# An audio tower on one core: three of five token tiles get their 128th-largest value by a bit search

## The chip, the cores and the metric

The kernel runs on 1 core of one Trainium2 chip. The metric is device microseconds for one launch over all 32 sequences; lower is better. Three runs of the kernel before took 9348.07, 9358.02 and 9363.74 us, median 9358.02. An engine is named as in the profile: PE (TensorE), PEld (its weight loads), DVE (VectorE), ACT (ScalarE), POOL (GpSimd), SP (the DMA queue).

## The reference

For each of 32 sequences of 80000 samples, 625 frames of 128 samples (padded to 626) go through a DCT and three residual blocks:

```
h = dct(frames)
h = h + bidirectional_mamba2(layernorm(h))        # 4 heads x 64, state 16, sequential scan over 626 steps
h = h + moe(layernorm(h))                         # 8 experts, top 2, hidden 512, gelu
h = h + window_attention(layernorm(h))            # 8 shifts, softmax over the shifts
h = h + sparse_ffn(layernorm(h))
```

and the last one, which the change touches, is

```
a1 = gelu(x @ ipT)            # 512 values;  keep the 64 largest, others 0
a2 = gelu(a1_kept @ pwT)      # 256 values;  keep the 128 largest, softmax over those kept
v  = softmax_kept @ pv        # 64 values
a3 = gelu(v @ owT)            # 512 values;  keep the 64 largest, others 0
out = a3_kept @ op
```

All in float32.

## The kernel before

A sequence is 626 tokens, in five tiles of 128 tokens (`TILES`). Work on one sequence is cut in three stages: stage 1 is DCT and the scan block, stage 2 the experts and the attention, stage 3 the sparse feed-forward block. The loop is a software pipeline over sequences: one pass does stage 1 of sequence b, stage 2 of b-1 and stage 3 of b-2; two passes ahead of it and two behind it are partial. Each engine's part of a stage is a generator that yields between steps, and a string of digits for each engine (`PE_ORDER`, `ACT_ORDER`, `DVE_ORDER`, `POOL_ORDER`) says, digit by digit, which stage's generator takes its next step. The order of work on an engine is therefore fixed by hand; engines meet only through semaphores, and an engine that waits holds all that stands behind it in its string.

What the change and the prediction touch:

- `take_top` (lines 1017 to 1034) picks the k largest of a row on DVE: each round is a MAX8 (line 1028, the eight largest) and a MATCH_REPLACE8 (line 1030, those eight overwritten), preceded by a small MATCH_VALUE_LOAD. 64 of 512 takes 8 rounds, 128 of 256 takes 16. Tiles go in groups of three and two; rounds of the tiles of a group alternate. It runs three times: on `a1` (K1 = 64), on `a2` (K2 = 128) and on `a1` again (K3 = 64). `select` (line 1039) then zeroes what was not taken; for `a2` line 1068 does that and sums the row.
- ACT in stage 3: the evacuations and Gelus of lines 794 to 821, and one Exp per tile (line 807). In stage 2 ACT makes 64 Gelus per sequence (line 768) between PE's first (line 564) and second (line 575) expert products; PE can be only two halves ahead of ACT.
- POOL: layer norms (lines 312 to 317), and the attention's softmax and value sums. Those are few and wide: line 369 subtracts over 5120 columns in one instruction, lines 373, 376 and 392 add over 2560, 1280 or 640 columns.
- The scan block of stage 1 has 12 steps (lines 474 to 497, 742, 894 to 905). In each, PE multiplies `Bw` with `Cs` (16 rows, 121 weight columns, line 474) and transposes two 128 x 121 pieces of `xs` (line 481), both into 121 partitions, makes the skip and the head products (lines 491, 497), and DVE scans (line 894) and weighs (lines 902, 905).

## Time and profile before

| | |
|---|---|
| median of 3 runs | 9358.02 us |
| the profiled execution | 9383.6 us |
| its span, first to last instruction | 9381.6 us |
| busy: DVE / PE / ACT / POOL | 8440.0 / 7197.0 / 3228.9 / 2332.9 us |
| mean granted PE clock | 0.792 |

A busy time is the sum of the engine's instructions in the span; the chain of waits is the path of work, followed back from the last instruction, that ended last. The granted clock is given as a share of 2.4 GHz: 1.00 is 2.4 GHz and 0.50 is 1.2 GHz.

### The profile page before, as it was taken

The numbers are of one execution on the slowest core, as the hardware profiler recorded it, in microseconds if no ns is written. First come the engines' busy times: TensorE is split into PE (matmuls) and PEld (weight loads), VectorE is DVE, ScalarE is ACT, GpSimd is POOL, SyncE is SP. The second block draws the span as 40 slices with busy tenths as digits, with TensorE's granted clock in tenths as the row PEclk, the third lists the DMA queues.
The fourth block names the chain that finished last, engine by engine and source line by source line (L and its number), as shares of the span: only waits on it lengthen the run. The fifth ranks groups of instructions, "written<-read, shape, count | busy, mean of one in ns | idle before, by whom it ended". The sixth has DMA issues, their size and how long they took to land.

```text
span 9381.6 us, 113931 instructions
## 1 busy us (share of the span) xinstructions
PE 7197.0 (77%) x35336; PEld 5130.3 (55%) x35336; DVE 8440.0 (90%) x23276; ACT 3228.9 (34%) x5649; POOL 2332.9 (25%) x1967
## 2 busy tenths in 40 slices
PE   6778787787787787877777877878877878777773
PEld 4555555555565565555555555555555555555552
DVE  2699989989999999998999899999989999989998
ACT  2233333333333333333333333333333343333331
POOL 1332212332122322123322223221233222232220
PEclk9778877778887788787788777787877888778875
DMA  1000000000000000000000000000000000000000
GB/s 53 14 16 14 6 12 16 16 16 11 5 16 16 16 14 6 12 16 16 16 14 4 14 16 16 14 8 10 16 16 16 14 6 12 16 16 16 10 5 3
DMA packets 95339, 128.48 MB, mean 14 GB/s; under 512 B 7600, under 2 KB 94096, under 8 KB 94096
## 3 DMA queue, kind: packets, MB, share of 16 engines
q1 hardware_dynamic: 94736, 120.71, 4.8%
q8 instruction: 345, 5.65, 0.3%
q14 instruction: 258, 2.11, 0.1%
HBM read 109.68 MB, written 11.01 MB: 13 GB/s over the span
## 4 chain that ended last, share of the span: by engine, by line
DVE 59%; PE 26%; issue 7%; ACT 4%; POOL 3%; DMA 0%; DVEq 0%; SPq 0%; POOLq 0%; ACTq 0%
DVE m L1028 17%; DVE work L1030 14%; PE pM L575 6%; PE pM L564 6%; DVE dtw L870 4%; DVE a L1030 3%; PE pS L497 3%; PE pS L491 3%; DVE a L1039 2%; DVE h L972 2%; DVE hid L982 2%; ACT hid L768 2%; PE pS L481 2%; DVE hid L993 2%; DVE stats L853 2%
## 5 line engine op out<-in xcount | busy, mean ns | idle before, releaser
L1030 DVE MATCH_REPLACE8 work<-m,work 128x256 f32<-128x256 f32 (+1 forms) x4192 | 2178.7, 537 | 0.0
L1028 DVE MAX8 m<-work 128x8 f32<-128x256 f32 (+1 forms) x4192 | 2035.1, 539 | 1.0
L564 PE MATMUL pM<-uT,cst 128*128 128x320 f32 x4096 | 1495.2, 493 | 313.3 <-ACT hid L768 173.5
L768 ACT ACTIVATE hid<-pM,cst 128x320 f32<-128x320 f32 x2048 | 1060.3, 528 | 1247.8 <-PE pM L564 641.8
L463 PE MATMUL pS<-u_fm,wconv_s 128*128 128x315 f32 (+1 forms) x3072 | 1027.7, 496 | 498.6 <-DVE dtw L870 380.8
L575 PEld LDWEIGHTS pM<-cst,hid 128*128 128x128 f32 x10240 | 1185.8, 191 | 125.9 <-DVE h L972 80.6
L564 PEld LDWEIGHTS pM<-uT,cst 128*128 128x128 f32 x4096 | 724.2, 206 | 967.9 <-ACT hid L768 784.2
L575 PE MATMUL pM<-cst,hid 128*128 128x128 f32 x10240 | 1204.8, 275 | 49.1 <-DVE h L972 47.2
L312 POOL TENSOR_TENSOR rstd<-vare,mhalf 128x5 f32<-128x5 f32 x160 | 187.4, 1171 | 4171.8 <-DVE vare L859 4171.8
L463 PEld LDWEIGHTS pS<-u_fm,wconv_s 128*128 128x128 f32 (+1 forms) x3072 | 585.8, 196 | 953.3 <-DVE dtw L870 398.4
L497 PE MATMUL pS<-Mt,Xw 121*64 121x121 f32 x3072 | 359.2, 376 | 313.8 <-DVE Mt L905 313.7
L742 ACT COPY xs<-pS 128x242 f32<-128x242 f32 x384 | 138.9, 362 | 1297.3 <-PE pS L497 1297.3
L1028 DVE MAX8 m<-a 128x8 f32<-128x512 f32 x768 | 507.4, 682 | 86.2 <-issue 83.3
L894 DVE TENSOR_TENSOR_SCAN ab<-ab,cst 121x488 f32<-121x488 f32 x384 | 552.0, 1437 | 20.3 <-DMA ab<-decay_rows 19.2
L369 POOL TENSOR_TENSOR hid<-hid,red 128x5120 f32<-128x5120 f32 x32 | 350.7, 10960 | 710.5 <-DVE red L988 710.5
L340 POOL TENSOR_TENSOR yg<-xs,zs 128x525 f32<-128x525 f32 (+1 forms) x256 | 194.4, 799 | 1137.8 <-ACT xs L742 1107.4
L972 DVE SCALAR_TENSOR_TENSOR h<-pM,lgt,h 128x128 f32<-128x128 f32 x1280 | 361.6, 353 | 105.9 <-PE pM L575 100.2
L497 PEld LDWEIGHTS pS<-Mt,Xw 121*64 121x64 f32 x3072 | 233.0, 191 | 383.3 <-DVE Mt L905 320.2
L1030 DVE MATCH_VALUE_LOAD work<-m,work 128x8 f32 x4192 | 380.7, 91 | 0.0
L902 DVE TENSOR_TENSOR Xw<-pS,dts 121x256 f32<-121x256 f32 x384 | 159.2, 415 | 236.7 <-PE pS L481 236.2
L392 POOL TENSOR_TENSOR hid<-hid 128x2560 f32<-128x2560 f32 (+2 forms) x96 | 344.0, 3583 | 54.2 <-DVE hid L993 49.0
L1030 DVE MATCH_REPLACE8 a<-m,a 128x512 f32<-128x512 f32 x512 | 349.6, 683 | 0.0
(193 smaller groups left out, 12223.9 us busy)
## 6 DMA issues: line engine op xcount, KB each, us to landing
ab<-decay_rows SPq DMA_DIRECT2D x384, 230.7 KB
x_sb<-in_x SPq DMA_DIRECT2D x32, 256.0 KB
out<-hk SPq DMA_DIRECT2D x32, 256.0 KB
cst<-in_weights SPq DMA_DIRECT2D x2, 2048.0 KB, 12.0
hid<-in_setup SPq DMA_DIRECT2D x1, 1904.0 KB, 20.9
out<-hk SPq DMA_DIRECT2D x32, 57.0 KB
x_sb<-in_x SPq DMA_DIRECT2D x32, 56.5 KB
cst<-in_weights SPq DMA_DIRECT2D x1, 1344.0 KB, 17.0
```

The lines of the kernel that those rows point to most:

```text
L369: nc.gpsimd.tensor_tensor(lg, lg, red[:, 0:1, :].broadcast_to((P, AW, W)), ALU.subtract).then_inc(G["lg_done"].s, 1)
L392: nc.gpsimd.tensor_tensor(lg[:, 0:n, :], lg[:, 0:n, :], lg[:, n:2 * n, :], ALU.add).then_inc(G["val_tree"].s, 1)
L463: last = nc.tensor.matmul(pS[0:rows, 512 * (n % 3):512 * (n % 3) + HQ], wt, tap(d, i, half * HQ, HQ), start=(j == 0), stop=(j == len(block ...
L497: last = nc.tensor.matmul(pS[r * HD:(r + 1) * HD, B2 + g * WIN:B2 + (g + 1) * WIN], Xw[d][:, hh, :], Mt[d][:, hh, :], start=False, stop=(g ...
L564: nc.tensor.matmul(pM[:, 512 * (n % 2):512 * (n % 2) + W // 2], w1[:, e, j * P:(j + 1) * P], uT[:, lo:lo + W // 2], start=True, stop=True) ...
L575: last = nc.tensor.matmul(pM[:, B2 + P * (m % 4):B2 + P * (m % 4 + 1)], hid[:, e % 2, j, tok(t)], w2[:, e, j, :], start=(j == 0), stop=(j ...
L768: nc.scalar.activation(hid[:, e % 2, j, lo:lo + W // 2], pM[:, 512 * (n % 2):512 * (n % 2) + W // 2], ACT.Gelu, bias=c("b1")[:, n // 2:n / ...
L870: nc.vector.scalar_tensor_tensor(dtw[:, 1, :], dtw[:, 0, :], -1.0, dtw[:, 0, :], ALU.mult, ALU.max).then_inc(G["dt_arg"].s, 1)
L894: nc.vector.tensor_tensor_scan(decays, decays, c("scan_src", WIN), 0.0, ALU.mult, ALU.add).then_inc(G["scanned"].s, 1)
L972: last = nc.vector.scalar_tensor_tensor(h2[:, t, :], pM[:, B2 + P * (m % 4):B2 + P * (m % 4 + 1)], gate[:, t, e:e + 1], h2[:, t, :], ALU.m ...
L1028: link(nc.vector.max(m[i], now[i]), len(tiles) - 1)
L1030: link(nc.vector.match_replace(work[i], m[i], now[i], GONE), len(tiles) - 1 if r or firsts is None else 0)
```

## The change

`e2` now stands for tiles 3 and 4 only; tiles 0 to 2 (`SEARCHED = 3`) do not go through the 16 rounds on `a2`. For these three, a fourth generator, `search`, on ACT and POOL finds the 128th-largest value of each row bit by bit. In a turn, ACT makes three Sign passes over 257 columns (one per tile, sign of `flip * a2 + guess`, the sum of the signs into `below`), and POOL answers with three small instructions on 128 x 3 integers that set or leave a bit of `guess`. There are 31 turns and a few passes more before and after (Square passes that count ties, an upper neighbour of the value). DVE then makes the mask from the marks: a scan that numbers the ties, a compare-and-add, and the masked product that was there before. The search has the digit 4 in the orders; all four orders are new.

```diff
+SEARCHED = 3
+BITS = 31
+TURN = (3, 4, 0, 1, 2)
-            for tiles in groups:
-                dve.wait_ge(G["a2_sb"].s, G["a2_sb"](b, tiles[-1] + 1))
-                yield from take_top(tiles, a2, K2, halves, best)
+            for t in there:                                   # tiles 0, 1, 2
+                last = nc.vector.max(best[:, t, :], a2[:, t, 0:NP_])
+            ...
+            yield from take_top(here, a2[:, :, 0:NP_], K2, halves, best)      # tiles 3, 4
+            ...
+            for t in there:
+                dve.wait_ge(G["missing"].s, G["missing"](b, 1))
+                dve.wait_ge(G["e2s"].s, G["e2s"](b, t + 1))
+                link(nc.vector.tensor_tensor_scan(untied[:, t, :], c("minus1").broadcast_to((P, NP_)), untied[:, t, :], 0.0, ALU.add, ALU.add))
+                link(nc.vector.scalar_tensor_tensor(untied[:, t, :], untied[:, t, :], missing[:, t:t + 1], marks[:, t, 0:NP_], ALU.is_ge, ALU.add))
+                link(nc.vector.scalar_tensor_tensor(a2[:, t, 0:NP_], untied[:, t, :], 1.0, a2[:, t, 0:NP_], ALU.is_ge, ALU.mult,
+                                                    accum_out=rsum[:, t:t + 1]))
```

A turn on ACT, and its answer on POOL:

```diff
+            for n in range(BITS + 1):
+                yield
+                act.wait_ge(G["guess"].s, G["guess"](b, n + 2))
+                for t in range(SEARCHED):
+                    last = nc.scalar.activation(marks[:, t, :], a2[:, t, :], ACT.Sign, scale=flip[:, t:t + 1], bias=guess_f[:, t:t + 1],
+                                                accum_out=below[:, 0, t:t + 1])
+                last.then_inc(G["counted" if n < BITS else "marks"].s, 1)
```

```diff
+            for n in range(BITS):
+                yield
+                pool.wait_ge(G["counted"].s, G["counted"](b, n + 2))
+                wide = 1 << (BITS - 1 - n)
+                nc.gpsimd.tensor_tensor(raised[:], guess[:], halves_i[:, n:n + 1].broadcast_to((P, SEARCHED)), ALU.add)
+                nc.gpsimd.tensor_scalar(bit[:], below[:, 0, :], 1.0, float(wide), ALU.is_ge, ALU.mult).then_inc(G["tried"].s, 1)
+                pool.wait_ge(G["tried"].s, G["tried"](b, n + 1))
+                nc.gpsimd.tensor_tensor(guess[:], raised[:], bit[:], ALU.subtract).then_inc(G["guess"].s, 1)
```

Stage 3 now goes through its second half twice, first for tiles 3 and 4 and then for 0, 1 and 2 (`TURNS`). The wide POOL instructions of the attention become one instruction per 640 columns (8, 4, 2 and 4 + 2 + 1 of them):

```diff
-            nc.gpsimd.tensor_tensor(lg, lg, red[:, 0:1, :].broadcast_to((P, AW, W)), ALU.subtract).then_inc(G["lg_done"].s, 1)
+            for w in range(AW):
+                last = nc.gpsimd.tensor_tensor(lg[:, w, :], lg[:, w, :], red[:, 0, :], ALU.subtract)
+            last.then_inc(G["lg_done"].s, 1)
```

In the scan block `Bw` has 128 columns and the transposed pieces of `xs` too, so that these three PE products of a step write 128 partitions, where 121 are used:

```diff
-                nc.tensor.matmul(pS[0:WIN, at:at + WIN], Bw[d][:, ch, :], Cs[d][:, ch, :], start=True, stop=True)
+                nc.tensor.matmul(pS[:, at:at + WIN], Bw[d][:, ch, :], Cs[d][:, ch, :], start=True, stop=True)
-                    last = nc.tensor.transpose(pS[0:WIN, at + P + g * P:at + P + (g + 1) * P], xs[d][:, g, ch * WIN:(ch + 1) * WIN], ident)
+                    last = nc.tensor.transpose(pS[:, at + P + g * P:at + P + (g + 1) * P], xs[d][:, g, ch * WIN:ch * WIN + P], ident)
```

The new orders, cut to their first digits where they are long:

```
ACT_ORDER   278 digits (243 before), of them 41 fours, the first after 35 twos (16 of the 64 expert Gelus), the 32nd after 121
POOL_ORDER  "2334444444444141444444444444444444444444242222211222121141"
DVE_ORDER   119 digits (132 before)
PE_ORDER    227 digits (225 before)
```

## Rows read from the trace of the kernel before

**Rows 1.** The page: busy time of each engine.
```profile
PE 7197.0 (77%) x35336; PEld 5130.3 (55%) x35336; DVE 8440.0 (90%) x23276; ACT 3228.9 (34%) x5649; POOL 2332.9 (25%) x1967
```

**Rows 2.** The page: the chain that ended last, by engine and by line.
```profile
DVE 59%; PE 26%; issue 7%; ACT 4%; POOL 3%; DMA 0%; DVEq 0%; SPq 0%; POOLq 0%; ACTq 0%
DVE m L1028 17%; DVE work L1030 14%; PE pM L575 6%; PE pM L564 6%; DVE dtw L870 4%; DVE a L1030 3%; PE pS L497 3%; PE pS L491 3%; DVE a L1039 2%; DVE h L972 2%; DVE hid L982 2%; ACT hid L768 2%; PE pS L481 2%; DVE hid L993 2%; DVE stats L853 2%
```

**Rows 3.** Timeline, POOL's first instruction of stage 3 (start us, us).
```profile
392.36 1.25 POOL L400 TENSOR_TENSOR hk<-h,zero 128x640 f32<-128x640 f32 x1
...
8959.39 1.25 POOL L400 TENSOR_TENSOR hk<-h,zero 128x640 f32<-128x640 f32 x1
```

**Rows 4.** Windows of one pass: start:end length, PE, PEld, DVE, ACT, POOL busy, PEclk, DMA, GB/s.
```profile
4302.90:4326.90 24.00, 13.57 (x63) 9.66 (x61) 23.92 (x25) 4.23 (x9) 19.33 (x8) 0.81 0.06 21
...
4375.00:4399.10 24.10, 14.83 (x56) 9.75 (x56) 14.24 (x64) 6.29 (x10) 17.88 (x26) 0.65 0.06 16
...
sum 288.60, PE 225.51 PEld 161.49 DVE 264.04 ACT 101.00 POOL 72.79; mean PE 18.79 PEld 13.46 DVE 22.00 ACT 8.42 POOL 6.07
```

**Rows 5.** Windows: the expert stage of one pass, and the scan steps.
```profile
4094.00:4234.00 140.00, 113.63 (x588) 82.16 (x586) 127.45 (x456) 56.16 (x101) 12.41 (x18) 0.87 0.01 3
...
4326.00:4362.00 36.00, 35.98 (x180) 28.38 (x181) 26.46 (x44) 4.46 (x12) 0.16 (x1) 0.50 0.25 62
```

**Rows 6.** Groups by form: one replace per tile and round, 256 columns.
```profile
L1030 DVE MATCH_REPLACE8 work<-m,work 128x256 f32<-128x256 f32 x2400 | 975.6, 428 | 0.0
```

**Rows 7.** DVE timeline: two successive rounds of three tiles begin.
```profile
4175.80 1.07 DVE L1028 MAX8 m<-work 128x8 f32<-128x256 f32 x3
...
4177.96 1.07 DVE L1028 MAX8 m<-work 128x8 f32<-128x256 f32 x3
```

**Rows 8.** Timeline: DVE instructions beside wide POOL instructions, and without them.
```profile
4142.71 0.69 DVE L1039 SCALAR_TENSOR_TENSOR a<-work,a 128x512 f32<-128x512 f32 x1
...
4266.60 10.96 POOL L369 TENSOR_TENSOR hid<-hid,red 128x5120 f32<-128x5120 f32 x1 [22.42 <-DVE red L988]
4266.67 10.96 DVE L870 SCALAR_TENSOR_TENSOR dtw<-dtw 121x48 f32<-121x48 f32 x1
...
4282.96 0.21 DVE L884 SCALAR_TENSOR_TENSOR dts<-dtw 121x48 f32<-121x48 f32 x1
...
4299.76 3.23 DVE L1039 SCALAR_TENSOR_TENSOR a<-work,a 128x512 f32<-128x512 f32 x1
...
4315.42 4.35 DVE L894 TENSOR_TENSOR_SCAN ab<-ab,cst 121x488 f32<-121x488 f32 x1
...
4327.85 1.17 DVE L894 TENSOR_TENSOR_SCAN ab<-ab,cst 121x488 f32<-121x488 f32 x1
```

**Rows 9.** ACT timeline: three Exp passes of stage 3.
```profile
4188.60 1.31 ACT L807 ACTIVATE a<-a,nmax 128x256 f32<-128x256 f32 x3
```

**Rows 10.** Groups by form, ACT: a pass with and without a scale vector, table loads, Square.
```profile
L768 ACT ACT_TABLE_LOAD x94 | 120.6, 1283 | 3.7 <-PE pM L575 2.0
L817 ACT ACTIVATE a<-pD,rsum 128x512 f32<-128x512 f32 x160 | 109.9, 687 | 361.5 <-PE pD L658 361.1
L794 ACT ACTIVATE a<-pD 128x512 f32<-128x512 f32 x160 | 91.8, 595 | 200.8 <-PE pD L623 200.8
L747 ACT ACTIVATE zs<-yg 128x1280 f32<-128x1280 f32 x64 | 81.4, 1272 | 85.4 <-POOL yg L340 85.4
```

**Rows 11.** Groups by form: small POOL instructions, and the read of DVE's accumulator.
```profile
L312 POOL TENSOR_TENSOR rstd<-vare,mhalf 128x5 f32<-128x5 f32 x160 | 187.4, 1171 | 4171.8 <-DVE vare L859 4171.8
L315 POOL TENSOR_TENSOR tick_pool<-zero 128x1 f32<-128x1 f32 x160 | 39.9, 249 | 12.5
L392 POOL TENSOR_TENSOR hid<-hid 128x640 f32<-128x640 f32 x32 | 49.7, 1555 | 2.5
L1068 DVE DVE_READ_ACCUMULATOR a<-work,a 128x1 f32 x160 | 14.7, 92 | 0.0
```

More of the change, by code:

```diff
@@ L10 @@
 U32 = mybir.dt.uint32
+I32 = mybir.dt.int32
 AX = mybir.AxisListType
@@ L391, in pool_stage2 @@
                 pool.wait_ge(G["val_tree"].s, G["val_tree"](b, j + 1))
-                nc.gpsimd.tensor_tensor(lg[:, 0:n, :], lg[:, 0:n, :], lg[:, n:2 * n, :], ALU.add).then_inc(G["val_tree"].s, 1)
+                for w in range(n):
+                    last = nc.gpsimd.tensor_tensor(lg[:, w, :], lg[:, w, :], lg[:, w + n, :], ALU.add)
+                last.then_inc(G["val_tree"].s, 1)
             yield
@@ L818, in act_stage3 @@
-            for t in range(TILES):
-                yield
-                act.wait_ge(G["oT_ps"].s, G["oT_ps"](b, t + 1))
-                nc.scalar.copy(selT[:], pD[:, 0:512]).then_inc(G["oT_sb"].s, 1)
+                nc.scalar.activation(a2[:, t, 0:NP_], pD[:, 512:512 + NP_], ACT.Gelu).then_inc(G["a2_sb"].s, 1)
+            for i, t in enumerate(TURN[0:TILES - SEARCHED]):
+                yield
+                act.wait_ge(G["top2"].s, G["top2"](b, TILES))
+                nc.scalar.activation(a2[:, t, 0:NP_], a2[:, t, 0:NP_], ACT.Exp, bias=nmax[:, t:t + 1]).then_inc(G["e2"].s, 1)
@@ L1044, in select, with out @@
                 yield
-                dve.wait_ge(done.s, done(b, tiles[-1] + 1))
-            def out(t):
+                dve.wait_ge(done.s, done(b, first + len(tiles)))
+            def out(i):
                 yield
-                dve.wait_ge(G["fin_ps"].s, G["fin_ps"](b, t + 1))
+                dve.wait_ge(G["fin_ps"].s, G["fin_ps"](b, i + 1))
+                t = TURN[i]
                 nc.vector.tensor_tensor(hk[:, t, :], hk[:, t, :], pD[:, 512:512 + P], ALU.add).then_inc(G["out_sb"].s, 1)
-            groups = [range(0, 3), range(3, TILES)]
@@ L1053, in dve_stage3 @@
-            for tiles in groups:
+            here, there = range(SEARCHED, TILES), range(0, SEARCHED)
+            for tiles in (there, here):
                 yield
                 dve.wait_ge(G["a1_sb"].s, G["a1_sb"](b, tiles[-1] + 1))
-                yield from take_top(tiles, a1, K1, places(TILES - 2))
-                yield from select(tiles, places(TILES - 2), G["sel1"])
+                yield from take_top(tiles, a1, K1, places(SEARCHED))
+                yield from select(tiles, places(SEARCHED), G["sel1"], tiles[0])
@@ L1085, in dve_stage3 @@
-            for t in due:
-                yield from out(t)
+            yield
+            dve.wait_ge(G["a2_sb"].s, G["a2_sb"](b, SEARCHED))
+            nc.vector.memset(tick[:], 0.0)
+            for t in there:
+                last = nc.vector.max(best[:, t, :], a2[:, t, 0:NP_])
+            link(last)
+            nc.vector.tensor_scalar(nmax[:, 0:SEARCHED], best[:, 0:SEARCHED, 0], -1.0, None, ALU.mult).then_inc(G["top2"].s, SEARCHED)
+            yield
+            dve.wait_ge(G["a2_sb"].s, G["a2_sb"](b, TILES))
@@ L1087, in dve_stage3 @@
+            yield
+            dve.wait_ge(G["h3_kept"].s, G["h3_kept"](b, 1))
+            for i in range(len(here)):
+                yield from out(i)
+            yield
+            dve.wait_ge(G["a3_sb"].s, G["a3_sb"](b, TILES))
+            yield from take_top(there, a1, K3, places(SEARCHED))
+            yield from select(there, places(SEARCHED), G["sel3"], len(here))
+            for i in range(len(here), TILES):
+                yield from out(i)
             dve.sem_clear(link3)
```

276 lines of the change are left out of this document (174 added, 102 removed).

## The prediction, written before the changed kernel was run

> **What bounds the kernel now.** I read the page's busy times first [rows 1]: DVE is busy 90% of the span, PE 77%, ACT 34%, POOL 25%. The chain of waits says the same [rows 2]: 59% DVE, above all the two top-k instructions (17% and 14%), and 26% PE. So DVE bounds, with PE not far behind. Next the period: stage 3's first POOL instruction comes at 392.36 us for the first sequence and at 8959.39 for the 31st, so one pass takes 8567.0 / 30 = 285.6 us [rows 3]; the window of one pass that I cut is 288.6 long, with DVE busy 264.0, PE 225.5, ACT 101.0, POOL 72.8 [rows 4]. Then the stages of a pass. In the expert stage (140 us) DVE is busy 127.5, PE 113.6, ACT only 56.2 [rows 5]. In the scan steps PE is busy 35.98 of 36 us, at a granted clock of 0.50 (1.2 GHz), and DVE has 9.5 us of gaps. In the norms between blocks DVE is busy 14.2 of 24.1 us [rows 4]. Last, DVE's own time hides waits: a 121 x 48 instruction takes 10.96 us, exactly beside POOL's 10.96 us subtraction, where its like takes 0.21 us [rows 8]. The trace calls that busy.
>
> **The change part by part**, per pass.
>
> *Top-k on DVE.* 2400 replaces of 256 columns with 75 per sequence are five tiles by 15 rounds, and a first round reads `a2` [rows 6]. A round of three tiles starts every 4177.96 - 4175.80 = 2.16 us [rows 7]. Sixteen rounds: 34.6 us. Three MAX8 stay, 1.1 us. Removed: 33.5 us. Added for three tiles: a scan over 256 columns, at the undisturbed 1.17 us for 488 [rows 8] 0.61 us, and one compare-and-add over 256, about half of 0.69 us for 512 plus its start, 0.42; with the links 1.1 us a tile, 3.4 us. Net -30 us (both ends: 3 tiles at 0.9 to 1.8 us, so -31 to -28).
>
> *POOL in 640-column pieces.* What waits beside wide POOL instructions in a pass [rows 8]: line 870, 10.96 - 0.21 = 10.75; line 1039, 3.23 - 0.69 = 2.5 and 1.3 in the next one; a scan, 4.35 - 1.17 = 3.2. Sum 17.8 us. With pieces a DVE instruction can wait at most for the piece in front, 10.96 / 8 = 1.37 to 1.55 us [rows 11]. Perhaps three of them do and lose 0.7 to 1.5 us each. Gain 14 us, bounds 8 and 17. PE's projections, which stand behind line 870, start 9 us sooner with it. POOL pays: 21 pieces at 1.55 instead of 1.37 us are 4 us, in a POOL busy for a quarter of the time, beside DVE's top-k rounds; without that cover the attention is 4 us later.
> By the Trainium skill (GPSIMD Engine Reference, Key points) GpSimd shares its SBUF interfaces with VectorE instructions that have two SBUF inputs, and the trace agrees: MAX8 rounds beside POOL keep their time, line 870 (two inputs) does not. If that held for each small piece too, every two-input instruction in those 12 us would pay one piece, and the gain would be the 8 us above.
>
> *The search, on ACT.* Three passes over 256 columns with a bias vector take 1.31 us [rows 9]. A scale vector adds 687 - 595 = 92 ns to a pass [rows 10]; an accumulator read takes 92 ns on DVE [rows 11], and ACT's is not shown, bounds 0 and 0.3 us per pass. A turn's passes: 1.31 + 3 x 0.092 + 3 x 0.092 = 1.86 us, bounds 1.6 and 2.5. There are 36 groups of three passes: 67 us. ACT goes from 101 to 168 of some 255 us.
>
> *The search, on POOL.* A turn is three instructions with one wait between. The smallest two-input one takes 249 ns, the power on 128 x 5 takes 1171 ns [rows 11]. An integer add on 128 x 3 is no power; I take 0.25 each and 0.1 for each of two hand-overs and the wait, 1.05 us; bounds 0.8 and 3.7. A turn is then 1.86 + 1.05 = 2.9 us, bounds 2.4 and 6.2. 31 turns: 90 us.
>
> *Where the turns stand.* In ACT's order they lie among the expert Gelus, from the 16th to the 59th: 43 of 64. At the 140 us of the whole stage (in part before and after the Gelus, which take some 128 us) 43 Gelus took about 86 us. Thirty-one turns need 90, and the Gelus and copies between them (43 x 0.53 = 23 us and 5 us) fill POOL's answers, 31 x 1.05 = 33 us. ACT waits for POOL in a turn and holds Gelus behind it, for which PE waits. So the expert stage, where the removed rounds stood, does not get shorter: it stays at about 140 us. What shortens is the rest, as tile work of DVE can move into the stage's freed 30 us.
>
> *The rest of the pass* is 285.6 - 140 = 145.6 us. PE is busy 225.5 - 113.6 = 112 us in it. DVE has 264.0 - 127.5 = 136.5 in it; minus 14 (POOL) and minus up to 30 of moved work it has 93 to 100. So PE bounds the rest, at 112 us if packed without gaps; it had 33 us of gaps. I give it 3 us of gaps: 115.
>
> *128 columns in the scan steps.* Seven more columns per load and 48 such products a pass: under 1 us more. Whether the fuller products lift the clock of 0.50 no row shows: bounds +1 and -10 us (twelve steps of 3.25 us would fall to DVE's 2.2 us and hand-overs, 2.4). I take 0, the row that is: PE was already busy 35.98 of 36 us and still at 0.50 [rows 5], so seven in 128 columns is a small push.
> The Trainium skill (TensorE: Matmul & The Clock Gate, Part 4) says that a transpose does not count as busy time for the clock; two of the three widened products of a step are transposes. By it the widening gives nothing; without it the 10 us of the bound are open.
>
> *Sum.* Period 140 + 115 = 255 us, 30.6 less than 285.6. Thirty such passes: -918 us. The ends: the passes with stages 1 and 2 only, and 2 and 3 only, lose their POOL waits and some rounds, -30 us; the last stage 3 stands alone, took 182 us, and now has K1 (30), 33 turns (90), scan, weights and third product (25), K3 (30) and the outputs in a row, about +10. Profiled execution: 9383.6 - 918 - 20 = 8446 us. The median of the runs lies 25.6 us below the profiled time: 8420 us.
>
> **The rivals.**
> *Clock.* The widened products lift the scan steps to 1.00. Period 246, 8150 us. For it: all else in those steps is dense. Against: the row above.
> *The chain of stage 3.* The first half of stage 3, 33 turns in a row, then the second half for three tiles make one dependent chain: 30 + 10 + 95 + 25 + 30 + 10 = 200 us, without the waits in line for DVE and PE that others hold. If those cost another 70, the chain is the bound, and half of the gain is given back: period 271, some 8910 us. For it: the norm stretch shows DVE gaps of 10 us in 24 [rows 4] that are such chains. Against: the orders are free to put it first.
> *Slower: the turn.* The ladder decides from the point at which 31 turns outlast the 90 us by the 30.6 us gained, a turn of 3.9 us. That happens if the three POOL steps are like the power of 1171 ns (a turn of 5.4 us) or if a Sign pass needs another table than the Gelus around it: two loads of 1.28 us [rows 10] for a turn, 5.5 us. Either adds 78 us to the expert stage: period 333 us, 10800 us. Against: Square and the copies run behind any table without a load of their own at their lines [rows 10], and the power is the one slow POOL instruction.
> The Trainium skill (ScalarE: Activation LUTs, Table sets) says that cheap functions are in every set and names relu, copy, identity and abs; it does not name Sign there, though it gives Sign the same accuracy class as those. By the rule the loads stay away.
> *It moves nothing*: DVE's 44 us go and PE's waits take their place, all of them. PE has 60 us of gaps in a pass [rows 4], so this needs every gap to stay.
>
> **How the numbers follow.** The forecast has 0.55 (its own range 8250 to 8640), the clock 0.13, the stage-3 chain with half of the gain 0.20, no change 0.02, slower 0.10. A change of under 0.2%, 19 us, can't be told from none. Faster: 0.88, same 0.02, slower 0.10. The range that leaves out two in ten reaches from the clock case, 8120, to most of the chain case, 8850.
>
> **What would show it.** DVE busy falls to about 220 us a pass, lines 1028 and 1030 at 256 columns to two fifths; line 870 falls under 2 us. ACT's Sign groups of three take about 1.9 us and no table load stands before them; POOL's answer is about 1 us; ACT is busy 165 to 170 us a pass. The expert stage keeps its 140 us, the rest falls to 115. PE is busy over 85%, and the chain of waits has more PE than DVE. The scan steps stay at 0.50 and 3.2 us each. Wrong if a turn is over 3.9 us, if loads stand in front of the Sign passes, or if the granted clock in the scan steps rises.

## The result, and the profile after

The changed kernel takes 9048.24 us (median of 4 runs, 9036.43 to 9059.44) against 9357.11 before (4 runs, 9348.07 to 9363.74): a ratio of 0.967, 95% interval 0.9654 to 0.9687. It is faster, as forecast, but by 309 us and not by 937: 8420 was predicted, and 9048 lies outside the range that ended at 8850.

The page of the changed kernel, span and busy times, and the shares of the chain that ended last; they answer to [rows 1] and [rows 2].

```profile
span 9034.6 us, 123676 instructions
...
PE 6831.5 (76%) x35336; PEld 4900.9 (54%) x35336; DVE 6980.2 (77%) x18956; ACT 5064.2 (56%) x12534; POOL 3220.1 (36%) x5905
...
issue 30%; DVE 27%; PE 24%; POOL 13%; ACT 5%; POOLq 1%; DMA 0%; ACTq 0%; SPq 0%; DVEq 0%
```

Read it beside the forecast. DVE lost 1460 us, 45.6 a sequence; the 44 that were forecast are there. ACT gained 1835 us, 57 a sequence where 67 were forecast. But no engine is busy more than 77% of the span (PE was to be over 85%), and the chain has 30% "issue", time in which an engine waits for nothing that the profile shows. No single engine bounds the whole of this kernel.

The timeline of POOL's first instruction of stage 3, first and 31st sequence, in answer to [rows 3]:

```profile
370.94 1.25 POOL L431 TENSOR_TENSOR hk<-h,zero 128x640 f32<-128x640 f32 x1
...
8562.93 1.25 POOL L431 TENSOR_TENSOR hk<-h,zero 128x640 f32<-128x640 f32 x1
```

(8562.93 - 370.94) / 30 = 273.1 us a pass, 12.5 less than the 285.6 before, where 30.6 were forecast. One pass in two windows, from POOL's first instruction of stage 3 to the end of the last query, key and value product, which is called the expert stage here, and the rest (start:end length, busy us of PE, PEld, DVE, ACT, POOL, granted clock, DMA share, GB/s), in answer to [rows 4, 5]:

```profile
4193.38:4357.56 164.18, 131.74 (x680) 94.16 (x679) 125.50 (x404) 127.11 (x339) 32.86 (x123) 0.93 0.00 1
4357.56:4466.46 108.90, 80.20 (x428) 57.83 (x427) 92.50 (x188) 30.87 (x52) 67.86 (x61) 0.75 0.12 34
sum 273.08, PE 211.94 PEld 151.99 DVE 218.00 ACT 157.99 POOL 100.73; mean PE 105.97 PEld 75.99 DVE 109.00 ACT 78.99 POOL 50.36
```

Cut at the same places, a pass of the kernel before (4102.20 to 4391.78) has 151.9 and 137.7 us. Its passes differ, so the means over 27 passes of each trace say more: 150.6 and 135.0 us before, 164.2 and 108.9 now. (The prediction's window of 140 us lay a little differently.) So the rest shortened by 26 us, not far from the 30.6 forecast, and the expert stage, which was to keep its length, grew by 14. Inside the stage, windows of 21 us show who was short there:

```profile
4256.40:4277.40 21.00, 17.11 (x107) 13.62 (x106) 8.30 (x33) 19.23 (x57) 9.30 (x31) 1.00 0.00 0
4277.40:4298.40 21.00, 18.70 (x104) 14.04 (x104) 20.93 (x89) 19.64 (x56) 4.20 (x21) 0.92 0.01 2
4298.40:4319.40 21.00, 17.78 (x82) 10.39 (x80) 6.05 (x25) 19.91 (x55) 3.18 (x16) 1.00 0.00 1
```

ACT is busy 19.2 to 19.9 of 21 us while DVE falls to 8.3 and 6.1. An engine at 56% over the span is at 91 to 95% in these 63 us of the pass. Two turns back to back, ACT's timeline (start, us):

```profile
4241.57 0.53 ACT L843 ACTIVATE hid<-pM,cst 128x320 f32<-128x320 f32 x1
4242.30 0.60 ACT L909 ACTIVATE marks<-a,guess,flip 128x257 f32<-128x257 f32 x1 [0.21 <-POOL guess L449]
4242.81 0.19 ACT L909 ACTIVATION_READ_ACCUMULATOR marks<-a,guess,flip 128x1 f32 x1
4242.90 0.59 ACT L909 ACTIVATE marks<-a,guess,flip 128x257 f32<-128x257 f32 x1
4243.39 0.19 ACT L909 ACTIVATION_READ_ACCUMULATOR marks<-a,guess,flip 128x1 f32 x1
4243.49 0.59 ACT L909 ACTIVATE marks<-a,guess,flip 128x257 f32<-128x257 f32 x1
4243.98 0.19 ACT L909 ACTIVATION_READ_ACCUMULATOR marks<-a,guess,flip 128x1 f32 x1
4244.07 0.92 ACT L843 ACTIVATE hid<-pM,cst 128x320 f32<-128x320 f32 x2
4244.95 0.60 ACT L909 ACTIVATE marks<-a,guess,flip 128x257 f32<-128x257 f32 x1
```

A group of three takes 1.77 us, a turn here 2.65 us, and two Gelus fit exactly into POOL's answer: the turn is as forecast (2.9), and better packed. What it does to the Gelus shows in where the 64 of one pass stand, before and after (first and last start, us):

```profile
L768 ACT ACTIVATE hid<-pM,cst x64: 519/527/569, 4132.3 to 4224.4; 128x320 f32<-128x320 f32 x64
```
```profile
L843 ACT ACTIVATE hid<-pM,cst x64: 502/522/534, 4213.1 to 4334.2; 128x320 f32<-128x320 f32 x64
```

They took 92 us and now take 121. PE waits for them; the groups of PE's first expert product before and after (busy us, mean ns, idle us before and its releasers):

```profile
L564 PE MATMUL pM<-uT,cst 128*128 128x320 f32 x4096 | 1495.2, 493 | 313.3 <-ACT hid L768 173.5 <-DVE h L963 95.5
```
```profile
L636 PE MATMUL pM<-uT,cst 128*128 128x320 f32 x4096 | 1578.2, 503 | 617.2 <-ACT hid L843 481.3 <-DVE h L1072 117.3
```

The wait for ACT's Gelus, `hid`, was 173.5 us over the run, at 181 places; now it is 481.3, at 488.

### The profile page after: what moved, and what is told of

It reads as the page before. It is cut to its first block, busy times and chain, and to the rows that moved or that the text cites. A ratio compares the mean times of both kernels' runs of the same rounds, so it can differ in the third digit from the quotient of the medians.

```text
span 9034.6 us, 123676 instructions
## 1 busy us (share of the span) xinstructions
PE 6831.5 (76%) x35336; PEld 4900.9 (54%) x35336; DVE 6980.2 (77%) x18956; ACT 5064.2 (56%) x12534; POOL 3220.1 (36%) x5905
## 4 chain that ended last, share of the span: by engine, by line
issue 30%; DVE 27%; PE 24%; POOL 13%; ACT 5%; POOLq 1%; DMA 0%; ACTq 0%; SPq 0%; DVEq 0%
PE pS L535 8%; DVE m L1137 8%; DVE work L1139 5%; DVE a L1139 3%; POOL bit L447 3%; PE pM L636 2%; PE pD L710 2%; POOL raised L446 2%; POOL guess L449 2%; DVE ab L1003 2%; POOL u L339 1%; PE pM L647 1%; DVE red L1106 1%; PE pS L569 1%; DVE stats L962 1%
## 5 line engine op out<-in xcount | busy, mean ns | idle before, releaser
L636 PE MATMUL pM<-uT,cst 128*128 128x320 f32 x4096 | 1578.2, 503 | 617.2 <-ACT hid L843 481.3
L909 ACT ACTIVATE marks<-a,guess,flip 128x257 f32<-128x257 f32 x3072 | 1809.8, 592 | 230.9 <-POOL guess L449 194.8
L1139 DVE MATCH_REPLACE8 work<-m,work 128x512 f32<-128x512 f32 (+1 forms) x2752 | 1580.8, 581 | 0.0
L1137 DVE MAX8 m<-work 128x8 f32<-128x512 f32 (+1 forms) x2752 | 1499.1, 585 | 1.1
L446 POOL TENSOR_TENSOR raised<-guess,halves 128x3 int32<-128x3 int32 x992 | 206.2, 208 | 2238.4 <-ACT marks L909 2238.4
L535 PE MATMUL pS<-u_fm,wconv_s 128*128 128x315 f32 (+1 forms) x3072 | 868.5, 433 | 5.5 <-ACT Cs L804 5.5
L393 POOL TENSOR_TENSOR hid<-hid,red 128x640 f32<-128x640 f32 x256 | 518.9, 2059 | 606.7 <-DVE red L1097 606.7
L895 ACT COPY selT<-pD 128x512 f32<-128x512 f32 x160 | 93.8, 586 | 983.9 <-PE pD L742 983.2
L909 ACT ACTIVATION_READ_ACCUMULATOR marks<-a,guess,flip 128x1 f32 x3072 | 577.3, 188 | 0.0
L742 PE MATMUL pD<-cst,a 128*128 128x128 f32 x640 | 137.5, 354 | 432.0 <-DVE a L1148 385.6
L422 POOL TENSOR_TENSOR hid<-hid 128x640 f32<-128x640 f32 x224 | 338.6, 1536 | 173.6 <-DVE hid L1102 168.5
```

Source lines behind the costliest of these rows:

```text
L393: last = nc.gpsimd.tensor_tensor(lg[:, w, :], lg[:, w, :], red[:, 0, :], ALU.subtract)
L446: nc.gpsimd.tensor_tensor(raised[:], guess[:], halves_i[:, n:n + 1].broadcast_to((P, SEARCHED)), ALU.add)
L535: last = nc.tensor.matmul(pS[0:rows, 512 * (n % 3):512 * (n % 3) + HQ], wt, tap(d, i, half * HQ, HQ), start=(j == 0), stop=(j == len(block ...
L636: nc.tensor.matmul(pM[:, 512 * (n % 2):512 * (n % 2) + W // 2], w1[:, e, j * P:(j + 1) * P], uT[:, lo:lo + W // 2], start=True, stop=True) ...
L909: last = nc.scalar.activation(marks[:, t, :], a2[:, t, :], ACT.Sign, scale=flip[:, t:t + 1], bias=guess_f[:, t:t + 1], accum_out=below[:, ...
L1137: link(nc.vector.max(m[i], now[i]), len(tiles) - 1)
```

## Experiments

Ratios are to the kernel before on the same chip. "A pass" is the difference of two medians over 32 sequences; where it is a difference to the changed kernel, the two ran on different chips, on which the kernel before took 9357 to 9371 us, so it is good to some 0.4 us a pass. Of the 18 measured times two lie in a range that their expectation gave (a_expclock and a_two3, each in its rival's); the others lie between the ranges or beyond them.

One thing has to be known for all that follows. The passes of one run are not alike, although their instructions and orders are: the granted clock differs. In the kernel before, 18 of 28 passes in the middle of the run (first scan step to the next pass's first) start the last three of the twelve scan steps at 1.00 and take 284.1 us; the other 10 start them at 0.50 and take 288.7. An edit can shift how many passes are of which kind, and a gain or loss of 1 to 3 us a pass may be that shift.

### The change's parts alone

**b_pieces**: the kernel before with the attention's wide POOL instructions in pieces of 640 columns.

```
-  nc.gpsimd.tensor_tensor(lg, lg, red[:, 0:1, :].broadcast_to((P, AW, W)), ALU.subtract)
+  for w in range(AW):
+      last = nc.gpsimd.tensor_tensor(lg[:, w, :], lg[:, w, :], red[:, 0, :], ALU.subtract)
```

> The kernel before with only the four wide POOL instructions of the attention cut into 640-column pieces. Theory A (the waits of DVE beside wide POOL instructions are on the path): DVE's line 870 falls from 10.96 us to under 1.5 us and the run gains 8 to 17 us a pass, 240 to 500 us, 0.95 to 0.975 of before. Rival (the new orders are needed for it, PE and the scan steps take its place): line 870 falls, but the gain is under 90 us, over 0.99.

Measured: 9257.05 us, ratio 0.9888 (0.9871 to 0.9904), 3.3 us a pass. The groups of four DVE instructions of the decay chain, the row of small instructions ahead of the scan steps, show why it is so little (busy, mean ns):

```profile
L878 DVE SCALAR_TENSOR_TENSOR dtw<-dtw 121x48 f32<-121x48 f32 x32 | 47.6, 1488 | 1.1
L885 DVE TENSOR_TENSOR dtw<-dtw 121x48 f32<-121x48 f32 x32 | 46.0, 1436 | 1.1
L884 DVE TENSOR_SCALAR dtw<-dtw 121x48 f32<-121x48 f32 x32 | 45.3, 1416 | 1.1
L890 DVE TENSOR_TENSOR dtw<-dtw 121x48 f32<-121x48 f32 x32 | 45.3, 1416 | 1.1
```

Line 870, 10.96 us before [rows 8], is now 1.49 on average; but three of its successors, 0.2 us before, take 1.4 us, and two more 0.8 and 0.9: most of the chain pays for a piece of POOL. DVE is busy only 5.1 us a pass less. The prediction gave this case as the lower bound of the term, 8 us, and took 14. The clock hides a part: in 14 of 28 passes the last scan steps start at 1.00 (278.1 us), in 14 they do not (285.1). At like clock that is 6.0 and 3.6 us less than before, still under the bound.

**b_cols**: the kernel before with 128 columns in the three scan products.

```
-  nc.tensor.matmul(pS[0:WIN, at:at + WIN], Bw[d][:, ch, :], ...)        # 121 columns
+  nc.tensor.matmul(pS[:, at:at + WIN], Bw[d][:, ch, :], ...)            # 128
```

> The kernel before with only the scan step's products widened from 121 to 128 columns. Theory C (the fuller products raise the granted clock of the scan steps): those steps show 1.00 instead of 0.50 and take 2.4 instead of 3.25 us, up to 10 us a pass, 0.965 to 0.99 of before. Theory N (the width does nothing, the clock depends on the gap of PE ahead of the steps): the steps stay at 0.50 behind PE's 10 us gap and the time is within 0.3% of before.

Measured: 9318.78 us, 0.9951 (0.9934 to 0.9968), 1.4 us a pass. The third to the ninth step still start at 0.50 in every pass of the middle, but the transposes' weight loads are faster with 128 columns than with 121. First the kernel before, then b_cols:

```profile
L481 PEld LDWEIGHTS pS<-cst,xs 128*121 128x121 f32 x768 | 158.3, 259 | 77.8 <-ACT xs L742 70.4
```
```profile
L483 PEld LDWEIGHTS pS<-cst,xs 128*128 128x128 f32 x768 | 96.7, 177 | 77.8 <-ACT xs L744 70.4
```

More columns, less time. The two means mix clocks; at like clock a load takes 204 instead of 301 ns (0.50) and 141 instead of 182 (1.00). That is not the whole effect: in b_cols the last three steps start at 1.00 in all 28 passes, not in 18. Its pass of 283.3 us is some 0.8 us under the 284.1 of before at the same clock; the rest of the gain is the clock of those steps, and whether the 128 columns brought that about is not shown. The mean clock was 0.803 or 0.804 in all four runs, and 0.794 to 0.797 in the seven of the kernel before beside them. The prediction had costed the columns at nothing.

**a_wide**: the changed kernel with the wide POOL instructions back.

> The changed kernel with the POOL instructions of the attention wide again. Theory A: DVE's two-input instructions wait again for up to 11 us, and it loses 8 to 17 us a pass, 0.995 to 1.02 of before. Rival (in the changed kernel DVE has 55 us of slack a pass, so the waits are covered): within 0.5% of the changed kernel, 0.965 to 0.972 of before.

Measured: 9605.48 us, 1.0245 (1.0219 to 1.0271): 557 us over the changed kernel, 17.4 a pass, and slower than before. The timeline of a scan beside the wide instruction:

```profile
4359.21 11.80 POOL L392 TENSOR_TENSOR hid<-hid,red 128x5120 f32<-128x5120 f32 x1 [18.65 <-DVE red L1089]
...
4361.83 10.20 DVE L995 TENSOR_TENSOR_SCAN ab<-ab,cst 121x488 f32<-121x488 f32 x1
...
4372.97 1.07 PE L561 MATMUL pS<-Mt,Xw 121*64 121x121 f32 x8 [5.08 <-DVE Mt L1006]
```

In the change's orders the wide subtraction falls on the first scan, which takes 10.20 us instead of 1.17; PE pauses 5.08 us, and the steps behind that pause start at 0.50 in all 28 passes, seven of which the changed kernel starts at 1.00. From the first step's start to the last's are 49.6 us against 31.8, so the pause and the clock together make up the loss. The same edit is worth 3.3 us a pass in the old orders and 17.4 in the new: what a part is worth depends on the orders around it.

**a_121**: the changed kernel with 121 columns again.

> The changed kernel with 121 columns again in the scan step's products. Theory C: the first eight scan steps fall from 1.00 to 0.50 and cost 0.5 to 0.9 us more each, the run loses 4 to 10 us a pass, 0.98 to 1.00 of before. Theory N: the steps keep 1.00 because PE has no long gap ahead of them, 0.965 to 0.97 of before.

Measured: 9106.93 us, 0.9721 (0.9705 to 0.9737), 1.8 us a pass lost. The first eight scan steps run at a granted clock of 1.00 all the same. So the steps did speed up, which the prediction had called a sign of being wrong, but not by the columns. Of the loss only 0.2 us lies in the scan steps (32.0 us against 31.8); in the traces 2.3 us of it lie in the expert stage (166.5 against 164.2), which the edit does not touch and where the clock is at 0.50 for longer. Why it is, is not shown.

### What the search costs

**a_nosearch**: the changed kernel without the search: no Sign or Square pass, no answer of POOL; the marks are constants. Of the edit only the turns are shown.

```
-  for n in range(BITS + 1):
-      yield
-      act.wait_ge(G["guess"].s, G["guess"](b, n + 2))
-      for t in range(SEARCHED): ... ACT.Sign ...
```

> The changed kernel with the search left out: no Sign or Square passes and no answers of POOL (the marks stay constant), all else and the orders kept. Theory L (the search's work on ACT lengthens the expert stage): the expert stage falls from 164 to about 140 us and the pass from 273 to about 250, 8300 us. Rival S (the chain of stage 3 or PE sets the pass, the search is covered): over 8850 us.

Measured: 8575.26 us, 0.9157 (0.9139 to 0.9174). The search costs 473 us, 14.8 a pass. Without it the kernel lies 155 us above the forecast of 8420, not 628.

**a_cut**: as many passes and answers, but the passes read constants and no turn but the last waits for POOL.

```
-  act.wait_ge(G["guess"].s, G["guess"](b, n + 2))
+  act.wait_ge(G["counted"].s, G["counted"](b, n + 1))     # but for the last pass
```

> The changed kernel with the same passes on ACT and the same answers on POOL, but ACT's 31 turns read constants and do not wait for POOL. Theory L1 (it is the passes that occupy ACT, in front of the expert Gelus): a gain of under 6 us a pass, 8860 to 9050 us. Theory L2 (it is the wait for POOL's answer in each turn): the turns come when the order has them and it gains 15 to 25 us a pass, 8250 to 8600 us.

Measured: 8835.34 us, 0.9432 (0.9416 to 0.9448), 6.7 us a pass better than the changed kernel. Less than half of the search's price is the wait for the answer: the 31 turns take 90.1 us instead of 95.1.

**a_thin**: the third tile's pass left out of each turn, all waits kept.

```
-  for t in range(SEARCHED):
+  for t in range(SEARCHED if n == BITS else SEARCHED - 1):
```

> Changed kernel with the third tile's Sign pass left out of the 31 turns (its threshold is wrong; answers of POOL and all waits stay). ACT loses 31 passes of 0.59 us, 18 us a pass of the loop, and the chain of turns is up to 18 us shorter. Theory A (ACT's occupancy is what the Gelus wait for in the expert stage): as much again as the cut chain gave with its occupancy kept (6.7 us), or more, 6 to 10 us a pass: 8730 to 8860. Rival C (only the chain of turns counts, of which 43 us were cut there for 6.7): 18/43 of it, 2 to 4 us a pass: 8920 to 8990.

Measured: 8597.24 us, 0.9176 (0.9158 to 0.9194). Eighteen us of ACT's time a pass are worth 14.1: with two passes a turn the search is nearly free (8597 against 8575 without any). PE's expert product and ACT's Sign group in this kernel:

```profile
L638 PE MATMUL pM<-uT,cst 128*128 128x320 f32 x4096 | 1483.7, 480 | 352.3 <-ACT hid L845 207.0 <-DVE h L1074 117.3
L911 ACT ACTIVATE marks<-a,guess,flip 128x257 f32<-128x257 f32 x2080 | 1229.8, 594 | 197.7 <-POOL guess L450 159.9 <-POOL flip L442 27.2
```

PE's wait for the Gelus falls from 481.3 to 207.0 us, near the 173.5 before the change, while ACT's wait for POOL (159.9 against 194.8) hardly moves. That is theory A, and stronger than its range (6 to 10 us a pass): ACT was full in the expert stage, and the last third of its load cost nearly its whole length. The chain of turns (rival C, 2 to 4) does not explain it. Where the time lies, in means over 27 passes of each trace (us):

| kernel | expert stage | rest | 16th to 59th Gelu |
|---|---|---|---|
| before | 150.6 | 135.0 | 69.8 |
| changed | 164.2 | 108.9 | 94.5 |
| a_nosearch | 150.0 | 108.9 | 79.9 |
| a_cut | 158.6 | 108.8 | 88.7 |
| a_thin | 150.5 | 108.9 | 81.5 |

(The last column is over 23 passes.) The search costs nothing in the rest; its whole price lies in the stretch of the expert Gelus. There the 31 turns take 95.1 us, of which ACT is busy 86.9; in a_thin they take 81.9, of which 70.0.

### Was DVE's load the bound before?

**b_free**: the kernel before without 15 of the 16 rounds on tiles 0 to 2.

```
+  if rounds is not None and r >= rounds:
+      continue
```

> The kernel before, in which tiles 0 to 2 skip 15 of their 16 rounds on the 256 values (wrong values are kept, the work is left out); orders as before. If DVE's time is the path in the expert stage, 32 us a pass go: 8350 to 8450 us. If PE and ACT stand close behind there (PE was busy 114 of 140 us), half of it or less: 8800 to 9000 us.

Measured: 9387.53 us, 1.0019 (1.0009 to 1.0029). DVE's busy time falls by 1016 us, 32 a pass, more than the change takes, and the kernel does not get faster. A part of this is the clock: all 28 passes start the last three scan steps at 0.50 and take 286.7 us, 2.0 less than such passes before; that the faster kind no longer occurs takes it back. But 2 us are not 32. DVE's waits in this kernel say where the time went (us in total, times, longest):

```profile
DVE h L972 <- PE pM L575: 1028.3, 193, 14.7
DVE Xw L902 <- PE pS L481: 300.9, 277, 8.7
```

The wait for PE's second expert product was 100.2 us before and is 1028.3 now. In the old orders the expert stage is held by more than DVE's load: it is 148.8 us long without the rounds, 150.6 with them, and DVE waits for PE, which is itself busy only 113.6 of 140 us in it [rows 5]. That the order of the work is what it lacks is borne out by b_ord below, where the stage takes 141.3 us with all rounds in place.

**b_three**: pieces, 128 columns and the left-out rounds together, in the old orders.

> Kernel before, in its old orders, with the 640-column pieces, the 128 columns and without 15 of the 16 rounds on tiles 0 to 2 (left out, so their weights are wrong): all reliefs of the change and none of its costs. Theory O (reliefs are worth nothing without the new orders, PE ends the expert stage): the sum of the three alone, 9357 -106 -44 +20, 9180 to 9260. Rival F (freed DVE and short pieces help each other even in the old orders): 8900 to 9100.

Measured: 9123.65 us, 0.9734 (0.9713 to 0.9756). Pieces and columns multiplied give 0.984, so the freed DVE is worth 1% here, some 2 us a pass, as it was in b_free at like clock. This lies between the two expectations. All reliefs of the change in the old orders give 9124, in the new orders 8575 (a_nosearch): the new orders, together with the second half of stage 3 that they take in two turns, hold some 550 us.

**b_late**: the kernel before, one stretch of DVE's order turned round.

> The kernel before with DVE's order changed at one place: a top-k round and the reciprocal, which stood between the first two scans, come after the first and the second weighing. Theory G (PE's clock falls in the 10 us gap ahead of the scan steps and they then run at 0.50 though PE is busy without a break): the gap falls to 3 to 6 us, the clock stays at 1.00 in at least half of the steps, and it gains 3 to 8 us a pass, 0.97 to 0.99 of before. Rival: the steps show 0.50 whatever is ahead of them, within 0.3% of before.

Measured: 9429.5 us, 1.0063 (1.0043 to 1.0083). DVE waits 67 us less for PE's transposes of the scan steps (168.7 for 236.2), but its scans are busy 86 us more. From the second step's start to the third's are still 11.0 us (12.6 before), not the 3 to 6 that theory G asked for, and the steps behind start at 0.50. So the edit did not remove the gap, and the run does not test the theory.

### The clock in the scan steps

**a_clock**: two rounds of DVE's last top 64 moved behind the scan steps.

```
 DVE_ORDER   ...  1.21 1.22 -3.53- 1.23 1.24 -3.54- 1.25 1.26 1.27 3.55 3.56 1.28 +3.53 3.54+ ...
```
(stage.step; the second and the fourth are moved)

> Changed kernel with one edit: two steps of DVE's order (the first two rounds of the last top 64 of tiles 0 to 2) moved behind the last weighing of the scan steps. Theory G (PE's pause of 5 us at 4395 to 4400, made by these rounds, is what drops the granted clock to 0.50 for the last scan steps): the pause goes, all 12 steps run at 1.00 and about 2.2 us, 4 slow steps save about 4 us and the pause 3 to 5, of which the later top 64 takes back 4: period -2 to -5, 8890 to 9000. Rival T (the clock falls at that place whatever DVE does): last steps stay at 0.50 and 3.2 us, time 9040 to 9130.

Measured: 9206.01 us, 0.9831 (0.9814 to 0.9849), 4.9 us a pass worse than the changed kernel. Its trace around the pause:

```profile
4470.04 1.28 ACT L859 ACT_TABLE_LOAD   x1
...
4471.33 4.47 ACT L859 ACTIVATE hid<-hid 128x5120 f32<-128x5120 f32 x1
...
4475.71 0.34 ACT L817 COPY xs<-pS 128x242 f32<-128x242 f32 x1
...
4476.10 0.69 PE L553 MATMUL pS<-cst,xs 128*128 128x128 f32 x2 [4.18 <-ACT xs L817]
```

The pause is ACT's: the attention's exponential, 4.47 us in one instruction behind a load of 1.28, stands ahead of the copy that PE's next step needs. DVE's two rounds had stood in that pause and cost nothing there; moved away, they make the rest of the pass 3.9 us longer (112.7 for 108.9).

**a_exp**: the exponential in four pieces, with copies between them. **a_expclock**: the same, with the moved rounds.

```
-  nc.scalar.activation(lg, lg, ACT.Exp)
+  for w in range(0, AW, 2):
+      if w:
+          yield
+      last = nc.scalar.activation(lg[:, w:w + 2, :], lg[:, w:w + 2, :], ACT.Exp)
```

> Changed kernel; the attention's exponential on ACT (line 859, 128x5120, 4.47 us behind a table load of 1.28) cut into four of 1280 columns with a scan step's copy (line 817) between them, the first one a step earlier. In the changed kernel this exponential stands ahead of the copy of scan step 9, PE pauses 4.18 us for that copy and its clock falls to 0.50 for the last steps. Theory G (that pause is what drops the clock): no pause over some 1.5 us, clock 1.00 through all steps not broken by DVE's top-k rounds, period -3 to -8: 8790 to 8950. Rival T (the clock falls there anyway, or the rounds of DVE between the last steps pause PE as well): the pause alone goes, 8950 to 9040, the last steps at 3.2 us.

> The same, and two rounds of DVE's last top 64 moved behind the last weighing as in a_clock. If those two rounds only filled the shadow of the exponential (why a_clock lost 4.9 us a pass), then without the shadow moving them costs less: theory G 8750 to 8900, with all steps at 1.00 and about 2 us; rival T 9050 to 9150, as a_clock less the pause.

Measured: 9082.18 us, 0.9692 (0.9674 to 0.9711), and 9120.13 us, 0.9733 (0.971 to 0.9755): 34 and 72 us slower than the changed kernel. In a_exp the pause falls to 1.42 us, but what the clock then does differs from pass to pass. Nine of the twelve steps start at 1.00 in every one of the changed kernel's 28 passes; in a_exp it is ten in 9 passes, eight in 4 and seven in 15. Passes with ten take 272.2 us, passes with seven 276.2; in the rest alone 107.7 and 110.1. So the clock of these steps does cost time. What the kernel lost as a whole lies in the expert stage (165.8 us on average for 164.2; the rest has 109.2 for 108.9).

In a_expclock all twelve steps start at 1.00 in 20 of 28 passes, and the first start to the last is 24.8 us instead of 31.8. Still the rest of such a pass takes 109.0 us, as in the changed kernel: what the steps won, the moved rounds behind them took. In 7 other passes the clock fell behind the seventh step, after a pause of like length. What decides between the two, with the same instructions in the same order, stays open.

### Orders

**a_two**: the bit search for two tiles, the third back on DVE, with a few steps moved by hand. **a_two2**, **a_two3**: the same program, only the written orders differ. **a_ord**: the changed kernel with other orders. **b_ord**: no search at all; the kernel before with pieces, 128 columns and new orders.

```
-SEARCHED = 3                                   +SEARCHED = 2
-TURN = (3, 4, 0, 1, 2)                         +TURN = (2, 3, 4, 0, 1)
```

> Changed kernel with the bit search for two tiles (0 and 1) instead of three; the third tile's 128 come from eight-at-a-time rounds on DVE again, and a few steps of stage 3 are moved in the written orders to fit. ACT loses one of three passes in each of 35 groups (0.59 us each, about 21 us a pass of the loop), DVE gains 15 rounds of one tile (about 11 us). Theory A (ACT's occupancy and the turns it delays are what the expert stage lost): expert stage 164 -> about 154 us, period 273 -> 262 to 268, 8700 to 8900. Rival D (DVE, 218 of 273 busy, is as much a bound as ACT): no gain or a loss, 9050 to 9250, since DVE has 11 us more. Moved orders may themselves cost or bring some 3 us a pass.

Measured: 10208.5 us, 1.0898 (1.0878 to 1.0917), against both expectations. PE waits 536.0 us for DVE to empty the expert sums (43.0 in the changed kernel). a_two3 below, with the same load, has 80.6: it was the moved steps, and so the run tells nothing of ACT.

> The bit search for two tiles again, this time with the four written orders fitted to it: an event count of the program (its queues and semaphores, each line at its mean duration in the trace of the changed kernel) was searched for orders with a short period. Where a_two was lost to misfit orders, this shows what 35 groups of two passes in place of three are worth (ACT -21 us, DVE +11 us a pass of the loop). Theory A (ACT was saturated in the expert stage, the orders made a_two slow): the count gives 28 us a pass less than for the changed kernel; taken by half to whole, 8150 to 8600. Rival D (DVE's 11 us more bind): 8800 to 9100.

> The changed kernel, three tiles, with nothing but its four written orders replaced by ones found in the same way. Count: 13 us a pass less than with the change's orders. Theory A (saturated ACT sets the stage, orders can only spread it): half of it or more, 8600 to 8850. Rival S (a count without the clock and without shared ports cannot order this kernel): 8950 to 9300.

Measured: 10142.3 us, 1.0821 (1.0803 to 1.0839), and 10389.03 us, 1.1088 (1.107 to 1.1107): a kernel with nothing but its orders changed (and one scratch tile split in two), 15% slower. Two groups of a_ord's ACT loads, of 1246 in all where the changed kernel has 413:

```profile
L844 ACT ACT_TABLE_LOAD x406 | 520.9, 1283 | 26.2 <-PE pM L648 19.1
L808 ACT ACT_TABLE_LOAD x184 | 236.1, 1283 | 3.3
```

833 more loads of 1283 ns are 1069 of the 1341 us; with all of the difference put down to them a load costs 1.61 us. From a_two2 to a_two3, below, 681 loads fewer go with 1098 us less, 1.61 us again. That the loads are the cause is likely by this, not shown: a_two, with 413 of them, took 10208 us. The orders of before and of the change keep Gelu, Silu and Exp apart (440 and 413 loads); a_two3 and b_ord, below, have 507 and 501. By the Trainium skill (ScalarE: Activation LUTs, Table sets) calls are to be batched by set; the trace agrees, and here the written order decides it. The same page puts a load at about 2.7 us with its drain, which would make 2249 us of these 833; no more than 1341 were measured. In the trace of a_ord the instruction behind a load starts 1.31 us after the end of the one ahead of it, in nine of ten cases.

> The two-tile search once more, with orders found by a count that now charges each table load of ACT (2.3 us each; the orders of a_two2 and a_ord made 1188 and 1246 loads against 413, 33 us a pass of the loop) and the delay from an engine's end to its waiter. Count: 55 us a pass less than a_two had, about 25 less than the changed kernel; loads about 440. Theory A (saturated ACT was the cause, table loads spoilt a_two2): 8300 to 8700. Rival D (DVE's 11 us more, or the count still lacks what orders this kernel): 8950 to 9600.

> No bit search: the kernel before with the 640-column pieces and the 128 columns, and its four written orders fitted by the same count. Count: 28 us a pass less than the old orders give with the same two edits (those alone, 9357 -106 -44, about 9210). Theory O (the old orders, not DVE's load, kept the expert stage at PE's pace and the change's gain is largely its orders): 8400 to 8800. Rival S (DVE, 250 of 285 us busy, was the bound after all, or the count misleads): 9050 to 9400.

Measured: a_two3 9044.79 us, 0.9649 (0.9633 to 0.9665); b_ord 8919.56 us, 0.9515 (0.9499 to 0.9531). The first shows that a_two and a_two2 were lost to orders alone: the same work in another sequence, 1164 and 1098 us less. It is level with the changed kernel (its interval touches that one's), so two tiles were not shown to beat three; theory A's 8300 to 8700 was not reached either, the time lies in the rival's range, and whether better orders would reach the 8597 of a_thin stays open. The second is the fastest kernel measured that leaves nothing out, faster than the change by 129 us without any of its search. Its page:

```profile
PE 6973.5 (78%) x35336; PEld 5059.3 (57%) x35336; DVE 8108.5 (91%) x23276; ACT 3280.8 (37%) x5710; POOL 2627.2 (29%) x2481
...
DVE 56%; PE 31%; issue 6%; ACT 3%; POOL 3%; DMA 0%; DVEq 0%; SPq 0%; POOLq 0%; ACTq 0%
```

Against pieces and columns in the old orders (9220 us, by the product of their ratios) the new orders bring 300 us, nearly all of it in the expert stage (141.3 us, 150.6 in b_pieces). It missed its own range (8400 to 8800). DVE is busy 91% of it, as before; whether taking rounds off it would pay in these orders no run shows, and after b_free the share alone does not say.

## Why the prediction was wrong

**The expert stage: the step that failed.** The prediction put 31 turns, 90 us, into a stretch of 43 Gelus that "took about 86 us", and so kept the stage at its length. The 86 came from spreading the 64 Gelus over "some 128 us" of the stage. They do not take that: in the trace of before they stand in 92 us (the line of L768 above), and from the 16th to the 59th are 69.8. So turns of 90 us make this stretch some 20 us longer, not 4. With 70 in place of 86 the prediction's own sum gives a period of 275 us and, by 30 passes of 20 us, about 9020 us; 9048 was measured. That it comes so near is in part luck: these Gelus take 94.5 us now, 25 more, of which the new orders alone make 10 (79.9 in a_nosearch), and the other parts of the stage give 11 back, so that it grew by 14.

The turns themselves came out as costed (2.65 us back to back, 3.17 on average against 2.9; groups of three 1.77 us against 1.86; POOL's answer under 1 us), and so did ACT's work beside them (31 x 1.86 + 28 = 86 us in the prediction, 86.9 of 95.1 measured). An ACT that is 91% busy there sets the pace: a third of the passes less gives back 14.1 of the search's 14.8 us a pass (a_thin), the wait for POOL 6.7 (a_cut); the two overlap, and no sum of them is to be made. The prediction compared ACT's 168 us with a whole pass of 255. It is 158, and 127 of them lie in the expert stage.

**The bound.** "So DVE bounds" was read from 90% of the span and 59% of the chain. b_free refutes it: DVE relieved of 32 us a pass, ratio 1.0019. A chain with 59% DVE says who was last, not by how much. The sum did not build on it: it gave the stage itself nothing and took its gain from work moved into the freed time, which needs new orders.

**The rest of the pass** was forecast 30.6 us shorter and is 26. DVE's part is as forecast: 93 to 100 us, measured 92.9. PE's is not: it was to bound the rest with 112 us and 3 us of gaps, and is busy 80 of 109, with 29 us of gaps (34 before). Its work shrank instead, by 21 us: 9 us more of it now stand in the expert stage, and the clock was at 0.50 for 54 us and not for 73. That the size is near is luck; what sets the 109 us is not shown.

**POOL in pieces** was costed 14 (bounds 8 and 17) independent of the orders. It measured 3.3 in the old ones, outside the bounds, as most of the decay chain pays for a piece, the case that the prediction named as the lower bound, and 17.4 in the new ones, the clock of the scan steps included.

**128 columns**: 0 forecast, 1.4 to 1.8 us a pass measured. In b_cols 0.8 of it stands at like clock, where the weight loads are faster, and the rest is clock. The forecast that the scan steps stay at 0.50 was wrong: eight of twelve ran at 1.00, also with 121 columns (a_121). That this did not throw the forecast of the rest further off is luck.

**The ends** were to give 20 us. The last stage 3, alone, takes 221 us after 182 before, 39 more where 10 were forecast, and the last pass before it is 10.5 us longer; the first stage 3 begins 21.4 us sooner. 30 x 12.5 + 21.4 - 10.5 - 39 = 347 us, the difference of the two spans.

**The rivals.** "The chain of stage 3", period 271 and 8910 us, came nearest (273), though its mechanism is not what was found: the wait in the chain of turns is at most the 6.7 us of a_cut. The slower turn and its table load did not occur: no load stands before the Sign passes. That agrees with the Trainium skill's rule that cheap functions are in every set (ScalarE: Activation LUTs, Table sets), though it does not name Sign. The clock rival was right that the scan steps would speed up, and wrong in the cause.

## What to carry to other kernels

Before work is moved to an idle engine, read from the trace how long the stretch is into which it goes, and what that engine does there already: here 87 us of ACT's work went into a stretch of 70, in a pass in which ACT was idle for two thirds. A bound is shown by taking the load away and looking at the time, not by a busy share: 32 us a pass less on the busiest engine brought nothing, and reordering (8920 us) was worth more than the new algorithm (9048). Judge a piece of a change in the orders that it will live in: the same edit was worth 3.3 and 17.4 us a pass. And before a microsecond a pass is put down to an edit, look whether the passes of a run are of one kind, and compare passes at like clock.

## What the runs showed of the hardware

- ACT's accumulator read takes 188 ns but is hidden: passes of 257 columns with it start every 0.59 us.
- A transposing weight load of 128 columns takes 141 ns at a granted clock of 1.00 and 204 at 0.50, one of 121 columns 182 and 301 (b_cols, before). The load of 16 rows in the same steps gains nothing from 128 columns (255 and 254 ns).
- With the same instructions in the same order, the granted clock of the last scan steps was 1.00 in some passes of a run and 0.50 in others, 4.6 us a pass apart in the kernel before.
- A table load takes 1283 ns, and the next ACT instruction starts 1.31 us after the end of the one ahead of the load (a_ord).
- A DVE instruction of the decay chain that meets a POOL piece of 640 columns takes about 1.2 us on top of its 0.21 (four of them in b_pieces, one a TENSOR_SCALAR); a scan beside a wide POOL instruction took 10.20 us for 1.17.
- POOL's integer steps on 128 x 3 elements take 0.19 to 0.26 us on average.
